# Attention and feed-forward on one core: the eight PSUM banks shared out as 3 + 3 + 2 instead of 4 + 2 + 2, and projected chunks read one exp later

## What is computed

```python
# x: (B=2, S=2048, D=256); H=16 heads of K=64; FFN hidden 768
h = layernorm(x)
q, k, v = h @ Wq + bq, h @ Wk + bk, h @ Wv + bv
attn = softmax(q @ k.T / sqrt(K))                # per batch and head, 2048 x 2048
y = layernorm(h + (attn @ v) @ Wo + bo, eps=1e-3) * gamma + beta
x = x + layernorm(y)
x = x + layernorm(ffn(layernorm(x)))             # silu(gate) * up, then down
```

## Time and profile before

| | us |
|---|---|
| median of 3 runs | 3201.6 (3199.45 to 3202.89) |
| the profiled execution, its own time | 3200.07 |
| its span, first to last instruction | 3198.3 |
| busy PE / DVE / ACT / POOL | 2949.4 / 2638.3 / 2390.4 / 2296.0 |

### The profile page before, as it was taken

The page is one execution under the profiler, slowest core; times in us unless marked ns, Lnnn a source line. Parts: engine busy times, 40 slices in busy tenths (PEclk is TensorE's granted clock), DMA queues, the critical chain, the costliest instruction groups (busy, mean ns, idle before and its releaser), DMA issues. The chain is left out here.

```text
span 3198.3 us, 83116 instructions
## 1 busy us (share of the span) xinstructions
PE 2949.4 (92%) x33632; PEld 2129.6 (67%) x33632; DVE 2638.3 (82%) x4729; ACT 2390.4 (75%) x4587; POOL 2296.0 (72%) x1810
## 2 busy tenths in 40 slices
PE   5799999999999999968999999999999999788897
PEld 4466666666666666656666666666666666577775
DVE  5688888888888888866888888888888888488886
ACT  3588888888888888945888888888888889633322
POOL 4488888888888888845888888888888888513222
PEclk8899999999999999978999999999999999899998
DMA  3523222222222333115233333233333222212110
GB/s 102 142 60 65 63 63 63 63 63 63 63 63 63 64 65 91 24 52 155 49 65 64 66 65 66 63 66 66 65 67 65 64 61 68 80 66 73 53 40 20
DMA packets 211660, 214.04 MB, mean 67 GB/s; under 512 B 158672, under 2 KB 181328, under 8 KB 198992
## 3 DMA queue, kind: packets, MB, share of 16 engines
q1 hardware_dynamic: 211280, 208.79, 27.7%
HBM read 53.16 MB, written 37.88 MB: 28 GB/s over the span
## 5 line engine op out<-in xcount | busy, mean ns | idle before, releaser
L474 POOL TENSOR_TENSOR p_l<-p_f,p_h 128x512 f16<-128x512 f32 x1536 | 1926.0, 1275 | 423.0 <-ACT p_h L539 418.9
L586 DVE TENSOR_REDUCE mx<-ps_aux 128x1 f32<-128x512 f32 x2048 | 1351.5, 681 | 313.3 <-PE ps_aux L754 311.4
L538 ACT ACTIVATE p_f<-ps_score 128x512 f32<-128x512 f32 x2048 | 1288.6, 630 | 109.9 <-PE ps_score L767 71.5
L539 ACT ACTIVATE p_h<-ps_score 128x512 f16<-128x512 f32 x2048 | 1299.2, 635 | 0.0
L766 PE MATMUL ps_score<-q_hilo,k_hihi 128*128 128x512 f32 x2048 | 1193.7, 583 | 0.3 <-ACT p_h L539 0.3
L787 PEld LDWEIGHTS ps_ctx<-v_hi_one_lo,p_h 128*128 128x128 f16 x8192 | 747.3, 96 | 285.7 <-issue 270.9
L754 PE MATMUL ps_aux<-k_half,q_half 65*128 65x512 f16 x2048 | 813.0, 398 | 103.7 <-DVE mx L586 97.5
L787 PE MATMUL ps_ctx<-v_hi_one_lo,p_h 128*128 128x65 f16 x8192 | 872.0, 194 | 1.5 <-POOL p_l L474 1.4
L789 PE MATMUL ps_ctx<-v_hi_one_lo,p_h 128*128 128x64 f16 x8192 | 862.2, 195 | 0.0
L791 PE MATMUL ps_ctx<-v_hi_one_lo,p_l 128*128 128x65 f16 x8192 | 856.8, 192 | 0.0
L767 PE MATMUL ps_score<-q_hi_max,k_lo_one 65*128 65x512 f32 x2048 | 816.0, 398 | 0.0
(11 more groups left out here) (126 smaller groups left out, 2624.5 us busy)
## 6 DMA issues: line engine op xcount, KB each, us to landing
k_hihi<-hi_st SPq DMA_DIRECT2D x64, 512.0 KB, 8.7
v_heads<-v_new SPq DMA_DIRECT2D x64, 258.0 KB, 2.0
v_hi_one_lo<-v_heads SPq DMA_DIRECT2D x32, 516.0 KB, 9.4
q_hilo<-hi_st SPq DMA_DIRECT2D x32, 512.0 KB, 4.8
q_hilo<-lo_st SPq DMA_DIRECT2D x32, 512.0 KB, 6.6
q_hi_max<-hi_st SPq DMA_DIRECT2D x32, 512.0 KB, 4.6
k_lo_one<-lo_st SPq DMA_DIRECT2D x32, 512.0 KB, 6.7
heads<-ctx_n SPq DMA_DIRECT2D x128, 128.0 KB, 2.0
```

The source lines that it names most:

```text
L474: nc.gpsimd.tensor_tensor(p_l[:, r], p_f[:, r], p_h[:, r], ALU.subtract).then_inc(lo_pool, 1)
L538: nc.scalar.activation(p_f[:, r], ps_score[:, bank], ACT.Exp, scale=K ** -0.5)
L539: nc.scalar.activation(p_h[:, r], ps_score[:, bank], ACT.Exp, scale=K ** -0.5).then_inc(exp_done, 1)
L586: nc.vector.reduce_max(mx[:, blk % 2, tt, ch:ch + 1], ps_aux[:, bank], AX_X).then_inc(max_read, 1)
```

## The change

The scores get 3 banks instead of 4, and `ps_aux` gets 3 (`SIDE`) instead of 2. An item of `ps_aux` now waits for the one three before it, and `used` runs on through the whole program instead of being set anew at each prologue and pair of heads. The banks of both are counted by a number that runs on over heads. `TAKE_LAG` is 5: ACT takes a chunk or a turned tile behind the exps of step t + 5. The number of instructions of each kind is the same.

```diff
-RING = 4
+RING = 3
+SIDE = 3
...
-TAKE_LAG = 4
+TAKE_LAG = 5
...
-        ps_aux = ctx.enter_context(nc.psum_tensor("ps_aux", [P, 2, BLK], F32))
+        ps_aux = ctx.enter_context(nc.psum_tensor("ps_aux", [P, SIDE, BLK], F32))
...
-                    r, bank = t % PROBS, t % RING
+                    r, bank = t % PROBS, ((g + u) * STEPS + t) % RING
...
-                        take_chunk(g + u + 2, chunk, g * AUX + b * TURNS + PRO_AUX + k, k % 2)
+                        take_chunk(g + u + 2, chunk, side0 + k, (side0 + k) % SIDE)
...
-            dve.sem_inc(max_read, 2)
+            dve.sem_inc(max_read, SIDE)
...
-            used = []
-
-            def after_maxima(m):
-
-                used[:] = [(max_read, m + 1), (max_read, m + 2)]
+            used = [(max_read, k + 1) for k in range(SIDE)]
...
-                used.append((max_read, m + 3))
+                used.append((max_read, m + 1 + SIDE))
...
-                if opening:
-                    after_maxima(g0 * STEPS)
-                else:
-                    used[:] = [(x_split, b * TURNS - 1), (x_split, b * TURNS)]
+                a0 = g0 * AUX + b * TURNS
...
-                if u == 0:
-                    after_maxima(g * STEPS + 2 * KT)
+                side0 = g * AUX + b * TURNS + PRO_AUX
```

More of the change, by code:

```diff
@@ L529, in prologue @@
                     if kind == "chunk":
-                        take_chunk(g0 + a, c, a0 + m, m % 2)
+                        take_chunk(g0 + a, c, a0 + m, (a0 + m) % SIDE)
             def head(b, i, g, u, first, last, coming, n):
                 _, chunks, turns, n = side_items(u, last, coming, n)
+                side0 = g * AUX + b * TURNS + PRO_AUX
                 for t in range(STEPS):
-                    r, bank = t % PROBS, t % RING
+                    r, bank = t % PROBS, ((g + u) * STEPS + t) % RING
                     act.wait_ge(s_full, (g + u) * STEPS + t + 1)
@@ L540, in head @@
                     for chunk, k in chunks[t - TAKE_LAG] if t >= TAKE_LAG else ():
-                        take_chunk(g + u + 2, chunk, g * AUX + b * TURNS + PRO_AUX + k, k % 2)
+                        take_chunk(g + u + 2, chunk, side0 + k, (side0 + k) % SIDE)
                     for gr, c, k in turns[t - TAKE_LAG] if t >= TAKE_LAG else ():
-                        act.wait_ge(aux_full, g * AUX + b * TURNS + PRO_AUX + k + 1)
-                        nc.scalar.activation(xTh[:, c, gr * BLK:(gr + 1) * BLK], ps_aux[:, k % 2], ACT.Copy)\
+                        act.wait_ge(aux_full, side0 + k + 1)
+                        nc.scalar.activation(xTh[:, c, gr * BLK:(gr + 1) * BLK], ps_aux[:, (side0 + k) % SIDE], ACT.Copy)\
                             .then_inc(xh_ready, 1)
@@ L587, in maximum @@
                 if kt == KT - 1:
-                    dve.wait_ge(max_read, m + 1 + 2)
+                    dve.wait_ge(max_read, m + 1 + SIDE)
                     nc.vector.reduce_max(mrow[:, blk % 2], mx[:, blk % 2], AX_X).then_inc(max_step, 1)
@@ L675, in prologue @@
                     if kind == "max":
-                        maximum(g0, a, c, a0 + m, g0 * STEPS + a * KT + c, m % 2)
+                        maximum(g0, a, c, a0 + m, g0 * STEPS + a * KT + c, (a0 + m) % SIDE)
                         if c == KT - 1:
@@ L686, in head @@
                     for ahead, blk, k, number in maxima[t]:
-                        maximum(g + u + ahead, blk, k, g * AUX + b * TURNS + PRO_AUX + number,
-                                (g + u) * STEPS + 2 * KT + t, number % 2)
+                        maximum(g + u + ahead, blk, k, side0 + number,
+                                (g + u) * STEPS + 2 * KT + t, (side0 + number) % SIDE)
                     if t + LO_AHEAD < STEPS:
@@ L699, in head @@
                     for gr, c, k in turns[t - 3] if t >= 3 else ():
-                        low_x((b + 1) * TURNS + gr * DT + c, gr, c, ps_aux[:, k % 2], x_split)
+                        low_x((b + 1) * TURNS + gr * DT + c, gr, c, ps_aux[:, (side0 + k) % SIDE], x_split)
                     block_before = not (first and u == 0 and j == 0)
@@ L765, in score @@
                 keys, cols = slice(kt * P, (kt + 1) * P), slice(j * BLK, (j + 1) * BLK)
-                nc.tensor.matmul(ps_score[:, t % RING], kA[u][:, keys], qA[u][:, cols], start=True, stop=False)
-                nc.tensor.matmul(ps_score[:, t % RING], kB[u][:, keys], qB[u][:, cols],
+                nc.tensor.matmul(ps_score[:, (g * STEPS + t) % RING], kA[u][:, keys], qA[u][:, cols], start=True, stop=False)
+                nc.tensor.matmul(ps_score[:, (g * STEPS + t) % RING], kB[u][:, keys], qB[u][:, cols],
                                  start=False, stop=True).then_inc(s_full, 1)
@@ L833, in prologue @@
                                 pe.wait_ge(x_split, b * TURNS)
-                        project(g0 + a, c, m % 2)
+                        project(g0 + a, c, (a0 + m) % SIDE)
                     if kind == "max":
-                        max_tile(0, g0, a, c, g0 * STEPS + a * KT + c, m % 2)
+                        max_tile(0, g0, a, c, g0 * STEPS + a * KT + c, (a0 + m) % SIDE)
                 pe.wait_ge(pro_free, score_base(b) + VALUES + (TURNS if opening else 0) + RING)
@@ L847, in head @@
                     for ahead, blk, k, number in maxima[t]:
-                        max_tile((u + ahead) % 2, g + u + ahead, blk, k, (g + u) * STEPS + 2 * KT + t, number % 2)
+                        max_tile((u + ahead) % 2, g + u + ahead, blk, k, (g + u) * STEPS + 2 * KT + t, (side0 + number) % SIDE)
                     for gr, c, number in turns[t]:
@@ L854, in head @@
                         for k in range(TB):
-                            mm = nc.tensor.transpose(ps_aux[:, number % 2, k * P:(k + 1) * P],
+                            mm = nc.tensor.transpose(ps_aux[:, (side0 + number) % SIDE, k * P:(k + 1) * P],
                                                      x_all[:, gr, k, c * P:(c + 1) * P], ident[:, :])
@@ L865, in head @@
                         for chunk, number in chunks[t]:
-                            project(g + u + 2, chunk, number % 2)
+                            project(g + u + 2, chunk, (side0 + number) % SIDE)
                         weigh(u, g, t - 1)
```

## The result

| | before | after |
|---|---|---|
| median, us | 3200.5 (4 runs) | 3067.4 (3066.6 to 3069.1, 4 runs) |
| ratio | 1 | 0.9585 (0.9568 to 0.9601) |
| span of the profiled execution | 3198.3 | 3065.8 |
| a full head | 79.0 | 75.2 |

What follows compares the result with a forecast made beforehand. PE was taken to bound the heads, with short losses to the two-deep `ps_aux`. From 3200.1, -119 (heads), -12 (prologues) and +2 (batch starts) gave 3071, set as a median of 3072 us; range 3055 to 3130 (8 in 10).

Steps and rivals of the forecast that it cites:

- PE is the bound in the heads: Full heads: PE sets the pace, needing 74.7 us of the 79.0 a head takes if it never waited.
- Losses of 4.3 us a head: Full heads: PE loses 4.3 us each to the two-deep `ps_aux`, by start times; the wait list shows 97.5 us in all.
- The third bank takes them, 131 us less 12: Heads: a third `ps_aux` bank removes PE's losses, 131 us, of which 12 stay, so -119 us.
- the later read moves DVE's and POOL's work nowhere: Heads, chunk reads: PE's projection still sets the read's time with `TAKE_LAG` 5, so DVE's and POOL's chunk work stays put.
- 0.4 us a head left: Heads: DVE bursts longer than two tiles' room still reach PE, 0.4 us a head, 12 us over 30 heads.
- End of the prologues -12: Ends of both prologues: three banks shorten the chain of four chunks, 6 us each, -12 us, range -7 to -14.
- the two chains of the prediction: Prologue ends: chunk reads paced by POOL's low part, 2.63 us, or read plus projection, 2.45 to near 3.8, whichever is larger.
- Three score banks: 0 in the heads, +2 at the batch starts: Scores: the later read covers the lost bank in heads, 0; the eighth score of each batch comes 1.0 us later, +2.
- rival 1: Heads: DVE becomes the bound, a head takes 76.9 us, gain 63 us, time 3129; chance 0.13.
- 3: Heads: the third bank only stores tiles, DVE's rate sets the head, only the prologues give 12 us, 3190; chance 0.05.
- Rival 2: Behind chunks in the heads: the later read doesn't cover the third score bank, costing 56 us more, 3128; chance 0.05.
- Rival 4: Every pair of steps: the exp gate locks PE to ACT; at 0.2 us a pair it gives 3277, slower; chance 0.05.

Runs made afterwards that it cites:

- e4: The changed kernel with DVE's split of the next projection weights at step 27 of a head instead of step 24; 3056.8 us, ratio 0.9557.
- e1: The changed kernel with the chunk's read where it was (TAKE_LAG 4 instead of 5), three banks for each; 3109.0 us.
- e3: The changed kernel with two banks for the scores and four for maximum tiles and chunks (RING 2, SIDE 4, instead of 3 and 3); 3119.9 us.

## Why the prediction was right, and where it wasn't

The time was predicted as 3072 and is 3067.4. Point by point:

- **PE is the bound in the heads, its own pace is 74.7.** Right. Without any loss (e4) a head takes 74.85.
- **Losses of 4.3 us a head by start times, not the 97.5 us of the wait list.** Right: 117.5 us left the two rows of 15 and 16 heads, more than the wait list has at all.
- **The third bank takes them, 131 us less 12.** The sum is right, and e1 shows the third bank taking PE's waits for DVE away without the later read. What failed is the step that said that the later read moves DVE's and POOL's work nowhere, and so costs and gives nothing in the heads. Alone it gives 50 us: DVE's cast became 0.97 us shorter in 56 of 128 cases, since POOL's list ran ahead of it. Both edits remove the losses behind the second chunks, so their gains overlap, and on top of the later read the third bank brings 83. That this error left the sum alone is luck: the gain that the prediction didn't see was one that it had already counted for the bank.
- **0.4 us a head left.** The kind of cause was right, a burst of DVE longer than the room, and so was the size (0.34), but the size by luck: it was a choice between 0 and 4.3 with no place in mind. The place is the split of weights, whose 0.43 us turned to 1.41 by meeting GpSimd, which the prediction had nowhere.
- **End of the prologues -12.** Reads of chunks after:

```profile
1425.31 0.66 ACT L494 ACTIVATE qk_new<-ps_aux,b_cur 128x512 f32<-128x512 f32 x1
1428.09 0.69 ACT L494 ACTIVATE qk_new<-ps_aux,b_cur 128x512 f32<-128x512 f32 x1 [2.11 <-POOL lo_st L457]
1431.43 0.69 ACT L494 ACTIVATE qk_new<-ps_aux,b_cur 128x512 f32<-128x512 f32 x1 [2.65 <-PE ps_aux L741]
1434.10 0.69 ACT L494 ACTIVATE qk_new<-ps_aux,b_cur 128x512 f32<-128x512 f32 x1 [1.98 <-PE ps_aux L754]
```

Spacings of 2.8, 3.3 and 2.7, between the two chains of the prediction; 15.1 us became 8.8. From the first read to the first score it is 9.1 in place of 16.1, and in the first prologue 8.3 in place of 14.5: -13.
- **Three score banks: 0 in the heads, +2 at the batch starts.** Right in the heads, with the cover from the later read (e1 shows the cost without it), and nearly right at the starts. The first and the eighth score of batch one after:

```profile
134.75 0.47 PE L766 MATMUL ps_score<-q_hilo,k_hihi 128*128 128x512 f32 x1
...
140.56 0.50 PE L766 MATMUL ps_score<-q_hilo,k_hihi 128*128 128x512 f32 x1
```

They are 5.81 us apart, in batch two as well, and were 4.82 and 5.37 apart before: +1.0 and +0.4. The first heads gained less than the usual 3.9 us (1.6 and 2.6) also because they had fewer losses to give back.
- **Not foreseen:** the last head of batch one and the start of its prologue, up to the first chunk's read, took 3.8 us less, where I had expected nothing. No run takes this apart.
- **The rivals.** 1 and 3 fell: PE is busy 74.94 of 75.00 us in the heads, so DVE doesn't set their pace. The time of rival 1 was added up wrongly, too: 68.2 + 5.6 + 2.2 is 76.0 and not 76.9, a gain of 90 and a time of 3102, so it stood 30 us off the forecast of 3072 and not 57. Rival 2 has its mechanism in e1 (42 us for the 56), in a kernel without the moved read. Rival 4 is not seen, even with two score banks (e3).

## What to carry to other kernels

When an engine with idle time holds up the bound one, ask whether it lacks rate or room: an extra piece of work on it tells (on average 0.54 of 0.60 us showed with two banks, 0.24 with three), if it is tried at more than one place of the list. Banks can be moved from a buffer whose reader keeps up to one whose reader comes in bursts, if the waits that guard the smaller buffer are moved with it. When two edits remove the same losses, what each is worth depends on the order: the third bank gives 83 us behind the later read, and the two together 133. And an instruction that moves on one engine's list shifts what the others overlap: before saying that it moves nothing, look which engines that share something with it run at that moment.

## What was unexpected of the hardware

A VectorE cast of 128x512 float32 to half precision took 0.41 us when it began ahead of GpSimd's next instruction, and 1.38 us when GpSimd's subtraction of two 128x512 tiles was under way, ending 0.28 us after that; shortening GpSimd's instruction to one column brought 0.41 back. A subtraction of two 128x256 tiles on VectorE took 1.41 to 1.44 us in the heads of the changed kernel where GpSimd's had begun 0.01 to 0.04 us ahead of it, and 0.43 where GpSimd's began 0.17 behind it: a shift of 0.2 us decides on 1.0. Moved by three steps it took 0.45 on average. The reductions from PSUM kept their mean of 680 to 683 ns in all of these kernels.
